# Cross attention: the weighed values turned in 32x32 blocks on VectorE, and each large projection of a step split in two halves

## The chip, the cores and the metric

The kernel runs on one core of one Trainium2 chip. The metric is the device time of one execution in microseconds (us); lower is better. All data are 32-bit floats. TensorE multiplies and turns matrices into PSUM banks, VectorE and ScalarE read and write PSUM and SBUF, GpSimd works on SBUF, and the SyncE queue issues most transfers.

## The reference, cut to what matters

Three sub-layers run one after the other on 8 batches of 256 tokens of width 512: a gated delta rule, a cross attention, and a feed-forward part with a router. The change lies in the cross attention:

```python
q = split_heads(hidden_states @ Wq, q_len)          # 32 heads of 16
k = split_heads(hidden_states @ Wk, q_len)
v = split_heads(hidden_states @ Wv, q_len)
q = q * cos + _rotate_half(q) * sin
k = k * cos + _rotate_half(k) * sin
scores = jnp.maximum(q @ k.T * inv_sqrt_d + attention_mask, finfo.min)
attn_output = softmax(scores) @ v
a_k = split_heads(adapter @ Wk, adapter_len)        # adapter: 256 rows for each batch
a_v = split_heads(adapter @ Wv, adapter_len)
a_scores = jnp.tanh(gate) * softmax(q @ a_k.T * inv_sqrt_d)
attn_output = attn_output + a_scores @ a_v
return attn_output.reshape(bsz, q_len, hid) @ Wo
x = _layernorm(x + cross_attention)                 # then a router score for each token
```

The softmax sums are got by a matmul: between two heads' values stands a block of ones, so each product holds 16 columns of weighed values and 16 columns that repeat the sum. "kind" 0 is the attention over the tokens, kind 1 that over the adapter.

## The kernel before, in words

The main loop of the cross attention (`cross_phase`, lines 982 to 1540) has 128 steps, 16 for each of the 8 batches. Two steps (a group) make one 128-token by 128-feature tile of the attention output; four groups make one query tile, and a batch has two. A step takes four head pairs with one of the two heads each. Below, u is the step and d its number in the batch (u mod 16).

The order of TensorE's work in step u is written out by hand (`pe_all`, lines 1179 to 1233): the scores of step u+1 (four tiles at row groups 0, 32, 64, 96; L1187, banks s0 to s3), the transposes of the first two probability tiles (L1200, into banks t0 and t1), perhaps a piece of other work, the transposes of the other two tiles, perhaps a second piece, and the weighing of step u (32 small matmuls, L1215, into bank o). Those pieces (`early` and `late`, lines 1050 to 1080) make the projections of the next batch, or finish the output of the present one. All of them use one bank, p; a piece may start when the one before has been taken out of it (`wait_taken`).

- early pieces, between the transposes: "norm" at each even d, "turn" at d = 1 and 9, "count" at 3, "qt1" at 7, "kt0" at 11, "kt1" at 13, "spread" at 15.
- late pieces, behind the transposes (or between them where the step has no early piece): x0, x1, q0, q1 at d = 0 to 3, out at 4, qt0 at 5, ak0, ak1, k0, k1, v0, v1, av0, av1 at 6 to 13, out at 14.

q, k, ak are projections (8 matmuls of 128x256, L1123), v, av and out have 4 matmuls of 128x512 (L1129, L1176), qt and kt rotate (L1134), x turns tokens (L1139). A plain matmul of these shows as two instructions in the trace, a transpose as one.

How a group's output comes about before: ScalarE copies bank o to `mixed` (L1309) at the end of each odd step; in the next even step TensorE turns `mixed` with 4 transposes into bank p ("norm", L1161); VectorE takes reciprocals of the sums, multiplies by tanh(gate), scales both kinds and adds them into `attn` (L1333 to L1345). For each query tile TensorE turns `attn` with 4 transposes ("turn", L1165), ScalarE copies that to `attn_t` (L1263), and "out" multiplies it with Wo (L1176). VectorE adds the result to the tokens and takes their statistics (L1359 to L1363).

ScalarE's order in a step: copy of the first turned probabilities (L1282), take of the early piece, second copy, eight exponentials of step u+1 (L1276), take of the late piece, at d = 5 a square root for the layer norm (`root`, L1268), and at odd steps the copy of bank o. VectorE's order: running minimum and mask for the first probability tile of step u+1 (`tops`, L1428), copy (L1437), early take, second tile, second copy, the last two tiles, late take, and at d = 6 `rate` (layer norm and router score of the batch before, L1381 to L1397). At d = 0 VectorE runs `choose` (L1399 to L1416) first. SyncE loads the adapter of the next batch when av1 has been made (L1475, L1476), and GpSimd applies the rotation (L1524 to L1539).

Of the kernel before, what the change touches and what calls it, by code (L numbers as in the profile page):

```python
# [12 lines left out]
P = 128  # L13
# [968 lines left out]
def cross_phase(nc, sem_stack, used, tokens, ctx_dram, mask_dram, weights, tables, tables_loaded, ident, chosen_rows, choice_sources):  # L982
# [4 lines left out]
    with ExitStack() as stack:  # L987
        a = Space(nc, stack, "xa_", sem_stack)
        gains = a.sb("gains", [P, XT, 2, 4])
# [15 lines left out]
        attn = a.sb("attn", [P, 2, D])  # L1005
        attn_t = a.sb("attn_t", [P, KC, P])
# [43 lines left out]
        def early(u):  # L1050

            b, d = divmod(u, HALVES)
            if d % 2 == 0:
                return ("norm", u // 2 - 1) if u else None
            if d == 9:
                return "turn", QT * b
            if d == 1:
                return ("turn", QT * b - 1) if b else None
            if d == 15:
                return ("spread", b - 1) if b else None  # L1060
            if d == 3:
                return ("count", b - 2) if b > 1 else None
            return (EARLY[d], b + 1) if d in EARLY and b + 1 < B else None

        def late(u):

            b, d = divmod(u, HALVES)
            if d == 4:
                return ("out", QT * b - 1) if b else None
            if d == 14:  # L1070
                return "out", QT * b
            return (LATE[d], b + 1) if d in LATE and b + 1 < B else None

        def inner(u):

            return early(u) or late(u)

        def outer(u):

            return late(u) if early(u) else None  # L1080

        TAIL = [("norm", LAST // 2 - 1), ("turn", QT * B - 1), ("out", QT * B - 1), ("count", B - 2), ("spread", B - 1),
                ("count", B - 1)]
        order = [(what, 0) for what in PROJECT]
        for u in range(LAST):
            order += [use for use in (early(u), late(u)) if use]
        order += TAIL
        BY_DVE = ("qt0", "qt1", "kt0", "kt1", "norm", "out", "count")
# [22 lines left out]
        def pe_make(pe, use):  # L1111
            what, at = use
            bank = bank_of[use]
            wait_taken(pe, previous[use])
# [4 lines left out]
            def project(w, half, src):  # L1119
                for h in range(2):  # L1120
                    m = 2 * half + h
                    for k in range(KC):
                        mm = pe.matmul(bank[:, h * S:(h + 1) * S], w[:, k, m * P:(m + 1) * P], src[:, k, :],  # L1123
                                       start=(k == 0), stop=(k == KC - 1))
                return mm

            def values(t, src):
                for k in range(KC):
# [29 lines left out]
            elif what == "norm":  # L1158
                wait(pe, mixed_taken, at + 1)
                for n in range(4):  # L1160
                    mm = pe.transpose(bank[:, n * P:(n + 1) * P], mixed[:, n * P:(n + 1) * P], ident)  # L1161
            elif what == "turn":
                wait(pe, normed, XT * (at + 1))
                for k in range(KC):
                    mm = pe.transpose(bank[:, k * P:(k + 1) * P], attn[:, at % 2, k * P:(k + 1) * P], ident)  # L1165
# [7 lines left out]
            else:  # L1173
                wait_taken(pe, ("turn", at))
                for k in range(KC):
                    mm = pe.matmul(bank[:, :], attn_t[:, k, :], w_o[:, k, :], start=(k == 0), stop=(k == KC - 1))  # L1176
            mm.then_inc(made, 1)

        def pe_all(pe):
# [11 lines left out]
            def turn_probs(v):  # L1191
                for i in range(4):
                    if i == 2 and inner(v):
                        pe_make(pe, inner(v))
# [30 lines left out]
            for u in range(LAST):  # L1225
# [3 lines left out]
                if outer(u):  # L1229
                    pe_make(pe, outer(u))  # L1230
# [4 lines left out]
        def act_take(act, use):  # L1235
# [23 lines left out]
            elif what == "spread":  # L1259
                wait(act, ranked, NC * at)  # L1260
                op = act.activation(score_rows[:, :], bank[:, 0:S], ACT.Copy)
            else:
                op = act.activation(attn_t[:], bank[:].rearrange("p (k n) -> p k n", k=KC), ACT.Copy)  # L1263
# [6 lines left out]
        def act_all(act):  # L1270
# [19 lines left out]
            act.activation(gains[:].rearrange("p t h i -> p t i h"), gate_in[:].rearrange("p (t i h) -> p t i h", t=XT, i=4),  # L1290
                           ACT.Tanh).then_inc(gains_made, 1)
            exps(0)
            for u in range(LAST):
                copy(u, 0)
                if early(u):
                    act_take(act, early(u))
# [3 lines left out]
                if late(u):  # L1300
                    act_take(act, late(u))
# [13 lines left out]
        def dve_take(v, use):  # L1315
# [10 lines left out]
            elif what == "norm":  # L1326
                t, slot = at % XT, at // XT % 2
                blocks = bank[:].rearrange("p (k h i x d) -> p k h i x d", k=2, h=2, i=4, x=2)
                if at == 0:
                    wait(v, gains_made, 1)  # L1330
                wait(v, made, made_at[use])
# [767 lines left out]
```

## Time and profile before

| what | value |
|---|---|
| median of 3 runs | 2974.13 us (2973.5 to 2975.09) |
| the profiled execution, its own time | 2976.63 us |
| its span, first to last instruction | 2974.8 us |
| mean granted TensorE clock | 0.982 of full speed |
| busy over the span | TensorE 94%, weight loads 59%, VectorE 59%, ScalarE 47%, GpSimd 17% |

In the windows shown below the three lines are batch 0, batches 1 to 6, and batch 7 of the loop; behind the busy times (number of instructions in brackets) stand the granted TensorE clock, where 1.00 is full speed, the share of the DMA engines and GB/s.

Most of the page is about the whole span, of which the main loop of the cross attention is a third. So the loop is read from windows and timelines. Busy times of TensorE overlap (matmuls are pipelined): the time a piece takes is read from its start to the start of what follows.

### The profile page before, as it was taken

The page shows a single profiled execution, that of the slowest core. Times are in us where ns is not written, and L with a number is a line of the kernel's source. Part 1 is how long each engine was busy: PE and PEld are TensorE (multiplying, and loading weights), DVE is VectorE, ACT ScalarE, POOL GpSimd, SP SyncE. Part 2 cuts the span into 40 slices and gives each one's busy share as a digit, 9 for nine tenths or more (in the row PEclk, how much of TensorE's full clock was granted, in tenths as well). Part 3 has the DMA queues.
Part 4 walks back from the last instruction along what each step waited for, and adds up shares of the span by engine and source line. Part 5 has one row for each costly group of instructions (what it writes and reads, how often), then busy time and mean ns, then how long its engine had stood idle before and what let it go on. Part 6 is the DMA issues. An engine that isn't in the chain of part 4 may idle for free. (4 is left out here: it accounts for less than half of the span.)

```text
span 2974.8 us, 81892 instructions
## 1 busy us (share of the span) xinstructions
PE 2807.7 (94%) x34646; PEld 1760.9 (59%) x34646; DVE 1748.0 (59%) x4940; ACT 1384.1 (47%) x3313; POOL 503.5 (17%) x626
## 2 busy tenths in 40 slices
PE   6999999999999999999998889999999999977999
PEld 3565656565656555555555566666666566654466
DVE  4555555555555555565656266666767667676533
ACT  3343434343433334343433166666666666664131
POOL 1221212121212121212121210102111010200020
PEclk8999999999999999999998899999999999998999
DMA  5010110101101101011011000000000000000441
GB/s 179 22 45 7 37 33 26 38 13 30 34 13 30 45 19 41 16 31 33 13 30 59 19 12 12 1 12 1 12 12 1 12 1 12 1 2 11 156 208 64
DMA packets 96922, 100.10 MB, mean 34 GB/s; under 512 B 38192, under 2 KB 84528, under 8 KB 95408
## 3 DMA queue, kind: packets, MB, share of 16 engines
q1 hardware_dynamic: 96400, 94.35, 10.0%
q8 instruction: 276, 4.52, 0.6%
q14 instruction: 86, 0.70, 0.1%
q0 software_dynamic: 160, 0.52, 0.0%
HBM read 90.01 MB, written 4.85 MB: 32 GB/s over the span
## 5 line engine op out<-in xcount | busy, mean ns | idle before, releaser
L201 PE MATMUL dr_p<-x_t,dr_w_g 128*128 128x512 f32 x1536 | 740.1, 609 | 11.0 <-DMA dr_w_g<-in_w_in 7.6
L1276 ACT ACTIVATE xa_probs<-xa_probs,xa_low 128x256 f32<-128x256 f32 x1024 | 436.6, 497 | 45.6 <-DVE xa_low L1428 43.6
L201 PEld LDWEIGHTS dr_p<-x_t,dr_w_g 128*128 128x128 f32 x1536 | 268.2, 191 | 226.5 <-issue 216.4
L1428 DVE CUSTOM_DVE_ANT_0 xa_probs<-xa_s,xa_mask 128x256 f32<-128x256 f32 x512 | 213.8, 418 | 263.0 <-PE xa_s L1187 263.0
L1200 PEld LDWEIGHTS xa_t<-ident,xa_probs 128*128 128x128 f32 x2048 | 223.2, 142 | 132.2 <-issue 79.1
L635 DVE SCALAR_TENSOR_TENSOR dr_acc<-dr_p,dr_taps,dr_acc 128x510 f32<-128x510 f32 (+2 forms) x384 | 284.9, 742 | 23.2 <-ACT dr_acc L493 15.2
L1200 PE MATMUL xa_t<-ident,xa_probs 128*128 128x128 f32 x2048 | 286.9, 281 | 7.7 <-DVE xa_probs_t L1437 6.0
L1282 ACT ACTIVATE xa_probs_t<-xa_t 128x512 f32<-128x512 f32 x256 | 152.8, 597 | 250.7 <-PE xa_t L1200 249.1
L1428 DVE CUSTOM_DVE_ANT_0 xa_probs<-xa_s,xa_zeros 128x256 f32<-128x256 f32 x512 | 214.4, 419 | 0.0
L1437 DVE COPY xa_probs_t<-xa_t 128x512 f32<-128x512 f32 x256 | 176.3, 689 | 43.4 <-PE xa_t L1200 29.4
L1215 PE MATMUL xa_o<-xa_probs_t,xa_val 128*32 128x128 f32 x4096 | 140.7, 278 | 44.6 <-DVE xa_probs_t L1437 24.8
L853 POOL TENSOR_TENSOR dr_first<-dr_n_mat,dr_packed 32x256 f32<-32x256 f32 x128 | 92.1, 719 | 503.4 <-DVE dr_n_mat L761 497.8
L493 ACT ACTIVATE dr_acc<-dr_p,dr_taps 128x512 f32<-128x512 f32 x128 | 87.4, 683 | 181.4 <-PE dr_p L201 181.4
L1215 PEld LDWEIGHTS xa_o<-xa_probs_t,xa_val 128*32 128x32 f32 x4096 | 107.1, 110 | 100.1 <-issue 75.2
L1187 PE MATMUL xa_s<-xa_keys,xa_q_pair 32*128 32x512 f32 x1024 | 163.4, 656 | 1.7 <-DVE xa_low L1428 1.0
L1528 POOL TENSOR_TENSOR xa_raw<-xa_raw,cos 128x512 f32<-128x512 f32 x32 | 40.7, 1272 | 689.1 <-DVE xa_by_sin L1324 689.1
L264 PEld LDWEIGHTS dr_g<-dr_yx,dr_f_low 32*32 32x32 f32 x8192 | 83.2, 106 | 109.6 <-issue 61.9
L867 POOL COPY dr_x_half<-dr_yx 32x256 f32<-32x256 f32 x32 | 12.4, 386 | 726.9 <-DVE dr_yx L676 726.9
L378 PE MATMUL dr_m<-dr_wo_g,dr_gated 128*128 128x512 f32 x256 | 127.5, 622 | 0.1
L681 DVE TENSOR_TENSOR tokens<-tokens,dr_m 128x512 f32<-128x512 f32 x64 | 44.0, 687 | 138.5 <-PE dr_m L378 138.5
L254 PEld LDWEIGHTS dr_f<-dr_yx,dr_n_mat 32*32 32x32 f32 x8192 | 82.3, 105 | 64.4 <-DVE dr_yx L769 28.8
L550 ACT ACTIVATE dr_k_tok<-dr_f 128x256 f32<-128x256 f32 x32 | 12.3, 384 | 231.9 <-PE dr_f L243 231.9
(319 smaller groups left out, 4894.8 us busy)
## 6 DMA issues: line engine op xcount, KB each, us to landing
dr_alpha<-alpha_rows SPq DMA_DIRECT2D x64, 254.0 KB, 4.3
dr_w_g<-in_w_in SPq DMA_DIRECT2D x48, 256.0 KB, 5.7
dr_alpha<-alpha_rows SPq DMA_DIRECT2D x32, 256.0 KB, 5.5
ff_wide<-in_fw_qkv SPq DMA_DIRECT2D x8, 1024.0 KB, 14.6
x_t<-in_x_t SPq DMA_DIRECT2D x4, 1024.0 KB, 7.6
tokens<-in_x_tok SPq DMA_DIRECT2D x1, 4096.0 KB, 15.9
dr_wo_g<-in_w_out SPq DMA_DIRECT2D x8, 512.0 KB, 3.8
xa_ctx_b<-in_ctx_t SPq DMA_DIRECT2D x8, 512.0 KB, 3.8
```

The source lines that it names most:

```text
L201: mm = pe.matmul(bank[:, :], w_g[:, k, m, :], x_t[:, k, 2 * S * batch:2 * S * (batch + 1)], start=(k == 0), stop=(k == KC - 1))
L378: mm = pe.matmul(y_banks[n][:, :], gated[:, e, j, c * P:(c + 1) * P], wo_g[:, j, :], start=(j == 0), stop=(j == VH - 1))
L493: act.activation(acc[:, m % 2].rearrange("p e n -> p (e n)"), bank_p[m % 2][:, :], ACT.Copy, scale=taps[:, group, m, TAPS - 1:TAPS]).then_ ...
L635: v.scalar_tensor_tensor(out=to[:, :, d:S], in0=bank[:, :, 0:S - d], scalar=taps[:, group, m, TAPS - 1 - d:TAPS - d], in1=to[:, :, d:S], o ...
L853: op = g.tensor_tensor(first[i], n_mat[i, :, i], packed[i, LOW:LOW + 1, :].to_broadcast([TR, EA, TR]), ALU.mult)
L1187: pe.matmul(bank_s[i][:, :], q_pair[32 * i:32 * i + 32, par, t, h, q * P:(q + 1) * P], keys[32 * i:32 * i + 32, par, t].rearrange("p k n - ...
L1200: mm = pe.transpose(bank_t[i % 2][:, at:at + P], probs[:, v % 3, i, kind, kt * P:(kt + 1) * P], ident)
L1215: mm = pe.matmul(bank_o[32 * i:32 * i + 32, at:at + P], val[:, par, kind, kt, 4 * t + i, h:h + 2], probs_t[:, v % 2, i, kind, kt, :], star ...
L1276: op = act.activation(at, at, ACT.Exp, bias=low[:, v % 3, i, kind:kind + 1], scale=-1.0)
L1282: act.activation(probs_t[:, v % 2, 2 * m].rearrange("p k t n -> p (k t n)"), bank_t[0][:, :], ACT.Copy)\
L1428: op = dve.tensor_tensor_reduce(out=probs[:, v % 3, i, kind, :], in0=bank_s[i][:, kind * S:(kind + 1) * S], in1=mask[:, par, q, :] if kind ...
L1437: dve.tensor_copy(probs_t[:, v % 2, 2 * m + 1].rearrange("p k t n -> p (k t n)"), bank_t[1][:, :]).then_inc(copied[1], 1)
```

## The change

It turns the weighed values on VectorE (`v.transpose`, which turns each 32x32 block in its place) instead of on TensorE. `turn_mixed` turns bank o straight into `mixed`, one 128x512 instruction, in each even step behind the first copy; it takes the place of ScalarE's copy and of the "norm" piece. `share` does the old VectorE arithmetic on `mixed` in SBUF at the end of the same step, and then turns the 128x128 result in blocks once more, straight into `attn_t`, which is doubled; it takes the place of the "turn" piece and of ScalarE's copy. The gate's layout follows.

The pieces are dealt out anew. Each step has a place between the transposes (BETWEEN) and one behind them (BEHIND). The twelve large pieces of a batch (q, k, v, ak, av, out) are made in two halves, at two places that follow each other; the bank is waited for at the first half and handed on at the second. ak0 and ak1 move from d = 6 and 7 to d = 0 and 1, the two outs from 4 and 14 to 6 and 15, `root` from d = 5 to 7, `rate` from 6 to 8. The last group is turned and shared after the loop, behind `choose`.

```diff
-        LATE = {0: "x0", 1: "x1", 2: "q0", 3: "q1", 5: "qt0", 6: "ak0", 7: "ak1", 8: "k0", 9: "k1", 10: "v0", 11: "v1",
-                12: "av0", 13: "av1"}
-        EARLY = {7: "qt1", 11: "kt0", 13: "kt1"}
+        HALF = {"ak0", "ak1", "q0", "q1", "v0", "v1", "k0", "k1", "av0", "av1", "out0", "out1"}
+        BETWEEN = ("ak0", "ak1", "x0", "count", "q0", "q1", "out1", "qt1", "v0", "v1", "k0", "k1", "av0", "kt1", "av1", "out0")
+        BEHIND = ("ak0", "ak1", "x1", "q0", "q1", "qt0", "out1", "v0", "v1", "k0", "k1", "kt0", "av0", "av1", "spread", "out0")
...
-            elif what == "norm":
-                wait(pe, mixed_taken, at + 1)
-                for n in range(4):
-                    mm = pe.transpose(bank[:, n * P:(n + 1) * P], mixed[:, n * P:(n + 1) * P], ident)
-            elif what == "turn":
-                wait(pe, normed, XT * (at + 1))
-                for k in range(KC):
-                    mm = pe.transpose(bank[:, k * P:(k + 1) * P], attn[:, at % 2, k * P:(k + 1) * P], ident)
...
             else:
-                wait_taken(pe, ("turn", at))
-                for k in range(KC):
-                    mm = pe.matmul(bank[:, :], attn_t[:, k, :], w_o[:, k, :], start=(k == 0), stop=(k == KC - 1))
-            mm.then_inc(made, 1)
+                wait(pe, normed, XT * (at + 1))
+                for k in quarters_now:
+                    mm = pe.matmul(bank[:, :], attn_t[:, at % 2, k, :], w_o[:, k, :], start=(k == 0), stop=(k == KC - 1))
+            if last:
+                mm.then_inc(made, 1)
...
-                if u % HALVES == 5 and u > HALVES:
+                if ended(u, 1):
+                    act_take(act, ended(u, 1))
+                if u % HALVES == 7 and u > HALVES:
                     root(act, u // HALVES - 1)
-                if u % 2:
-                    g = u // 2
-                    wait(act, weighed, 8 * (g + 1))
-                    if g:
-                        wait(act, made, made_at["norm", g - 1])
-                    act.activation(mixed[:, :], bank_o[:, :], ACT.Copy).then_inc(mixed_taken, 1)
...
+        def turn_mixed(v, g):
+            wait(v, weighed, 8 * (g + 1))
+            v.transpose(mixed[:, :], bank_o[:, :]).then_inc(mixed_taken, 1)
+
+        def share(v, g):
+            t, tile = g % XT, g // XT
+            blocks = mixed[:].rearrange("p (k h q x d) -> p k h q x d", k=2, h=2, q=4, x=2)
...
+            for h in range(2):
+                op = v.reciprocal(shares[:, :, h], blocks[:, :, h, :, 1 - h, 0])
...
+            v.tensor_tensor(joined[:].rearrange("p q h d -> p h q d"), parts[:, 0], parts[:, 1], ALU.add).then_inc(norm_step, 1)
+            if t == 0 and tile >= 2:
+                wait(v, made, made_at["out", tile - 2])
+            wait(v, norm_step, 4 * g + 4)
+            v.transpose(attn_t[:, tile % 2, t, :], joined[:].rearrange("p q h d -> p (q h d)")).then_inc(normed, 1)
...
                 copy(u, 0)
+                if u and u % 2 == 0:
+                    turn_mixed(dve, u // 2 - 1)
+                if ended(u, 0):
+                    dve_take(dve, ended(u, 0))
                 if u + 1 < LAST:
                     tops(u + 1, 1)
                 copy(u, 1)
                 if u + 1 < LAST:
                     tops(u + 1, 2, 3)
+                if ended(u, 1):
+                    dve_take(dve, ended(u, 1))
+                if u and u % 2 == 0:
+                    share(dve, u // 2 - 1)
+                if u % HALVES == 8 and u > HALVES:
                     rate(dve, u // HALVES - 1)
```

## Rows read from the trace of the kernel before

**Rows 1.** Windows: from:to, length, busy us of PE, PEld, DVE, ACT, POOL; clock.
```profile
1713.14:1843.76 130.62, 121.67 (x1097) 82.33 (x1097) 81.56 (x352) 85.82 (x187) 19.38 (x14) 0.97 0.04 13
1843.76:2612.46 768.70, 727.09 (x6661) 489.85 (x6657) 520.55 (x2200) 521.78 (x1117) 105.77 (x77) 1.00 0.02 7
2612.46:2724.72 112.26, 88.93 (x954) 59.59 (x950) 82.89 (x357) 78.26 (x170) 0.00 (x0) 0.94 0.01 2
```

**Rows 2.** Timeline of TensorE, step u=57 (d=9): start, length, engine, work, idle.
```profile
2172.70 1.14 PE L1187 MATMUL xa_s<-xa_keys,xa_q_pair 32*128 32x512 f32 x8
2173.77 1.09 PE L1200 MATMUL xa_t<-ident,xa_probs 128*128 128x128 f32 x8
2174.70 0.60 PE L1165 MATMUL xa_p<-ident,xa_attn 128*128 128x128 f32 x4
2175.20 1.17 PE L1200 MATMUL xa_t<-ident,xa_probs 128*128 128x128 f32 x8
2176.21 3.62 PE L1123 MATMUL xa_p<-xa_x_b,x_t 128*128 128x256 f32 x16
2179.76 1.08 PE L1215 MATMUL xa_o<-xa_probs_t,xa_val 128*32 128x128 f32 x32
2180.77 1.14 PE L1187 MATMUL xa_s<-xa_keys,xa_q_pair 32*128 32x512 f32 x8
```

**Rows 3.** Timeline, the even step that follows (u=58, d=10; norm and v0).
```profile
2183.27 1.16 PE L1200 MATMUL xa_t<-ident,xa_probs 128*128 128x128 f32 x8
2183.58 0.27 DVE L1333 RECIPROCAL xa_shares<-xa_p 128x8 f32<-128x8 f32 x2
2184.60 0.29 DVE L1345 TENSOR_TENSOR xa_attn<-xa_parts 128x128 f32<-128x128 f32 x1
2184.62 3.70 PE L1129 MATMUL xa_p<-x_t,xa_x_b 128*128 128x512 f32 x8 [0.18 <-DVE xa_parts L1339]
2188.25 1.08 PE L1215 MATMUL xa_o<-xa_probs_t,xa_val 128*32 128x128 f32 x32
```

**Rows 4.** Timeline of TensorE: end of d=15, then d=0 and d=1.
```profile
1970.54 1.08 PE L1215 MATMUL xa_o<-xa_probs_t,xa_val 128*32 128x128 f32 x32 [0.87 <-DVE xa_probs_t L1437]
1971.55 1.39 PE L1187 MATMUL xa_s<-xa_keys,xa_q_pair 32*128 32x512 f32 x8
1979.24 1.44 PE L1187 MATMUL xa_s<-xa_keys,xa_q_pair 32*128 32x512 f32 x8
1985.09 1.39 PE L1187 MATMUL xa_s<-xa_keys,xa_q_pair 32*128 32x512 f32 x8
```

**Rows 5.** Timeline, the step with the square root's table load (d=6).
```profile
2145.59 1.39 PE L1187 MATMUL xa_s<-xa_keys,xa_q_pair 32*128 32x512 f32 x8
2147.11 1.28 ACT L1268 ACT_TABLE_LOAD   x1
2155.71 1.14 PE L1187 MATMUL xa_s<-xa_keys,xa_q_pair 32*128 32x512 f32 x8
```

**Rows 6.** Timeline of VectorE: first and last instruction of choose, then of rate.
```profile
1971.68 0.29 DVE L1402 CUSTOM_DVE_ANT_0 xa_weighted<-xa_score_rows,ident 128x128 f32<-128x128 f32 x1
1974.14 0.16 DVE L1416 TENSOR_SCALAR xa_chosen<-xa_rank 128x2 f32<-128x2 f32 x1
...
2154.16 0.15 DVE L1383 RECIPROCAL xa_ln_den<-xa_ln_den 128x2 f32<-128x2 f32 x1
...
2156.61 0.42 DVE L1396 TENSOR_TENSOR xa_diag<-ident,xa_score 128x256 f32<-128x256 f32 x1
```

**Rows 7.** Groups by line: busy us, mean ns of one, then idle before them.
```profile
L1437 DVE COPY xa_probs_t<-xa_t 128x512 f32<-128x512 f32 x256 | 176.3, 689 | 43.4 <-PE xa_t L1200 29.4
L1538 POOL TENSOR_SCALAR xa_q_pair<-xa_raw,halves 128x512 f32<-128x512 f32 x32 | 49.7, 1564 | 1.6
L1387 DVE TENSOR_SCALAR tokens<-tokens,xa_moments,xa_ln_den 128x512 f32<-128x512 f32 x16 | 8.0, 543 | 0.3
```

**Rows 8.** DMA issues by line: KB each, median us to landing.
```profile
xa_ctx_b<-in_ctx_t SPq DMA_DIRECT2D x8, 512.0 KB, 3.8
```

More of the change, by code:

```diff
@@ L1065, in late @@
[L1065 to L1082, printed above, removed]
+        HALF = {"ak0", "ak1", "q0", "q1", "v0", "v1", "k0", "k1", "av0", "av1", "out0", "out1"}
@@ new lines, in cross_phase, with named @@
+        BETWEEN = ("ak0", "ak1", "x0", "count", "q0", "q1", "out1", "qt1", "v0", "v1", "k0", "k1", "av0", "kt1", "av1", "out0")
+        BEHIND = ("ak0", "ak1", "x1", "q0", "q1", "qt0", "out1", "v0", "v1", "k0", "k1", "kt0", "av0", "av1", "spread", "out0")
+        def named(what, b):
+            if what[:3] == "out":
+                at = QT * b - int(what[-1])
+                return ("out", at) if at >= 0 else None
+            if what in ("spread", "count"):
+                at = b - (1 if what == "spread" else 2)
+                return (what, at) if at >= 0 else None
+            return (what, b + 1) if b + 1 < B else None
@@ new lines, in piece, with ended @@
+        def piece(u, behind):
+            b, d = divmod(u, HALVES)
+            what = (BEHIND if behind else BETWEEN)[d]
+            use = named(what, b)
+            if not use:
+                return None
+            if what not in HALF:
+                return use, True, True
+            whole = list(itertools.chain.from_iterable(zip(BETWEEN, BEHIND)))
+            is_first = whole.index(what) == 2 * d + behind
+            return use, is_first, not is_first
+        def ended(u, behind):
+            made_here = piece(u, behind)
+            return made_here[0] if made_here and made_here[2] else None
@@ L1083, in cross_phase @@
+        TAIL = [("out", QT * B - 1), ("count", B - 2), ("spread", B - 1),
                 ("count", B - 1)]
@@ L1085, in cross_phase @@
         for u in range(LAST):
-            order += [use for use in (early(u), late(u)) if use]
+            for behind in range(2):
+                here = piece(u, behind)
+                if here and here[1]:
+                    order.append(here[0])
         order += TAIL
-        BY_DVE = ("qt0", "qt1", "kt0", "kt1", "norm", "out", "count")
+        BY_DVE = ("qt0", "qt1", "kt0", "kt1", "out", "count")
         made_at, taken_at, bank_of, previous = {}, {}, {}, {}
@@ L1109, in place, with pe_make @@
             return g // (QT * XT) % 2, q, t, v % 2
-        def pe_make(pe, use):
+        def pe_make(pe, use, first=True, last=True):
             what, at = use
             bank = bank_of[use]
-            wait_taken(pe, previous[use])
+            halves_now = [h for h in range(2) if (first, last)[h]]
+            quarters_now = [k for k in range(KC) if (first, last)[k // 2]]
+            if first:
+                wait_taken(pe, previous[use])
             if use == ("x0", B - NC):
@@ L1192, in turn_probs @@
                 for i in range(4):
-                    if i == 2 and inner(v):
-                        pe_make(pe, inner(v))
+                    if i == 2 and piece(v, 0):
+                        pe_make(pe, *piece(v, 0))
                     wait(pe, exped, 4 * v + i + 1)
@@ L1258, in act_take @@
                                     bank[:].rearrange("p (a h d) -> p a h d", a=PAIRS, h=2), ACT.Copy)
-            elif what == "spread":
+            else:
                 wait(act, ranked, NC * at)
                 op = act.activation(score_rows[:, :], bank[:, 0:S], ACT.Copy)
-            else:
-                op = act.activation(attn_t[:], bank[:].rearrange("p (k n) -> p k n", k=KC), ACT.Copy)
             op.then_inc(taken_act, 1)
@@ L1325, in dve_take @@
                                 sin[:, None, :].to_broadcast([P, 2, S]), ALU.mult).then_inc(taken_dve, 1)
[L1326 to L1331, printed above, removed]
-                for h in range(2):
-                    op = v.reciprocal(shares[:, :, h], blocks[:, :, h, :, 1 - h, 0])
-                op.then_inc(norm_step, 1)
-                wait(v, norm_step, 2 * at + 1)
-                v.tensor_tensor(shares[:, 1], shares[:, 1], gains[:, t], ALU.mult).then_inc(norm_step, 1)
-                wait(v, norm_step, 2 * at + 2)
-                for h in range(2):
-                    op = v.tensor_tensor(parts[:, :, h], blocks[:, :, h, :, h, :],
-                                         shares[:, :, h, :, None].to_broadcast([P, 2, 4, XD]), ALU.mult)
-                op.then_inc(taken_dve, 1)
-                wait_taken(v, use)
-                if t == 0 and at >= 2 * XT:
-                    wait(v, made, made_at["turn", at // XT - 2])
-                v.tensor_tensor(attn[:, slot, t * P:(t + 1) * P].rearrange("p (i h d) -> p h i d", i=4, h=2),
-                                parts[:, 0], parts[:, 1], ALU.add).then_inc(normed, 1)
             elif what == "count":
```

59 lines of the change are left out of this document (27 added, 32 removed).

## The prediction

> **What bounds the kernel now.** I looked at the busy slices of the page first: the loop of the cross attention is the part where TensorE shows 8 to 9 tenths. The windows then say how the loop splits: batch 0 takes 130.6 us, batches 1 to 6 together 768.7, that is 128.1 each, batch 7, which has no projections to make, 112.3 [rows 1]. In batches 1 to 6 TensorE is busy 727 of 769 us, VectorE 521, ScalarE 522. So TensorE bounds, and the clock it was granted is 1.00 of full speed, the 2.4 GHz level; in batch 7 it is busy only 79% and does not bound.
>
> The timeline says what a step costs on TensorE, from start to start [rows 2]: scores 1.07 us (2172.70 to 2173.77), two transposed tiles 0.93, "turn" 0.50, two tiles 1.01, k1 3.55, weighing 1.01; sum 8.07, without a hole. The step without pieces is 8.07 - 0.50 - 3.55 = 4.02 us.
>
> Holes are elsewhere, and I name them, since the change moves them:
> - In a step with "norm" the late piece waits until VectorE has scaled out of bank p: from the second transposes (2183.27) to v0 (2184.62) it is 1.35 us in place of 1.01, a hole of 0.34 [rows 3].
> - Step d=0 takes 7.69 us (1971.55 to 1979.24) for 4.02 + 0.50 norm + 0.50 x0 = 5.02 of work, so 2.67 of hole, 0.34 of it the one above: VectorE begins with choose, 2.6 us [rows 4, 6].
> - Step d=1 takes 5.85 for 5.02 of work, 0.8 of hole; where nothing stands behind the transposes (d=15, and d=5 has the same form) the weighing waits 0.87 for VectorE's copy [rows 4].
> - d=6 takes 10.12 (2145.59 to 2155.71) where a norm step with a large piece takes 8.5: ScalarE loads the square root's table (1.28 us) and the other one back, 1.6 of hole [rows 2, 3, 5].
>
> **The change, part by part, for a batch of 1 to 6.** What goes:
> - eight norms on TensorE, 8 x 0.50 = 4.0 us, and the holes behind them, 8 x 0.34 = 2.7;
> - two turns, 2 x 0.50 = 1.0;
> - the hole of the table load, 1.6: `root` is at d=7 now, in whose step and the next TensorE has 1.8 us more in each of the places around it. ScalarE, freed of the copy of bank o too, ends its eight exponentials some 3.9 us behind the third transpose, the root at 5.5, its next copy at 6.1; TensorE wants that copy only at 7.05 (rest of transposes 0.45, half a v 1.8, weighing 1.01, scores 1.07, transposes 0.93, other half 1.8). Were this cover gone, 1.6 would come back;
> - the holes of d=0, 1, 5 and 15: 2.3 + 0.8 + 0.9 + 0.9 = 4.9, less what I put in below.
> Sum 14.2 of 128.1, all of it on TensorE's path. ScalarE's copies of `mixed` and `attn_t` lie beside TensorE's work and bring nothing themselves.
>
> What comes:
> - Splitting. The change from transposes to a projection costs 1.01 - 0.93 = 0.08 us for the 256-wide kind [rows 2], and v0 with its 3.63 is 0.08 above k1's 3.55 [rows 3], so 0.16 for the 512-wide: 6 x 0.08 + 6 x 0.16 = 1.5 us.
> - VectorE. A turn of 128x512 out of PSUM does not occur in the trace. From below the bound is 0.54, a scaling of that shape inside SBUF; from above 1.56, GpSimd's slowest of that shape; the nearest row is the copy of that shape from PSUM, 0.69 [rows 7]. I take 0.69. For the 128x128 turn I take 0.29 as for the addition of that shape [rows 3], bounds 0.2 to 0.5. The old arithmetic takes 1.31 (2183.58 to 2184.89), so `share` is 1.6 and an even step holds 8 x 0.35 (running minima) + 2 x 0.69 + 0.69 + 1.6 = 6.5 us of VectorE in 7.6 of TensorE. In an ordinary even step nothing is late: counting from the start of the scores, VectorE's first tile is done at 2.0, the copy at 2.9, the turn at 3.6, the second tile at 4.3, and the fourth transpose, for which the second copy waits, ends only at 4.75. `share` stands behind the last minima, and only the next step's first tile waits for it (8.6 against 8.9).
> - New holes, where VectorE's queue is longer. d=0: choose and out0's take (three instructions, 1.6) push its first copy to 4.9 where TensorE wants it at 4.25, 0.65. d=9: share and rate (2.9 us [rows 6]) before it, the copy at 5.4 instead of 4.25, 1.15. d=2, now the light step (x0 and x1 alone, 5.0 of work): the turn delays the second copy, 1.05; d=3 behind it 0.5, since bank p and ScalarE's exponentials come late. d=14 has only "spread" behind its transposes, 0.4, and d=15 behind it 0.25. Sum 4.0.
> - DMA and the other queues: the adapter's load is issued when av1 is made, now at d=14 instead of 13, and ak0 wants it at d=0 instead of 6. From issue to need there are some 12 us, it lands in 3.8 [rows 8], so it costs nothing; SyncE's queue holds only the mask behind it, whose condition is older. If it took 20 us, each us over 12 would be on the path. GpSimd's rotations get the same order and steps before.
> So a batch changes by -14.2 + 1.5 + 4.0 = -8.7 us; six of them -52.
>
> Batch 0 loses 7 norms and a turn (7 x 0.84 + 0.5 = 6.4) and its light steps' holes, gains splits and ak0 in the first step, where everything waits and the clock is low: -6. In batch 7 even steps stay light: the norm's 0.50 and VectorE's 1.3 before the second tile give way to a turn of 0.69, but share follows; per pair of steps -0.3, with the root's hole -2 in all, bounds -8 and +5. Behind the loop two sets of four transposes and two ScalarE copies leave the chain and two turns enter it: -1. Sum -52 - 6 - 2 - 1 = -61 us. On the profiled execution, 2976.6 (2.5 us above the median), this is 2915.6; on the median, **2913**.
>
> **A rule weighed.** A copy from PSUM of the turn's shape takes 0.69 us, and four TensorE transposes take 0.50 [rows 2, 7]. The Trainium skill, "VectorE: DVE Perf Modes", section "The three transpose paths", gives 311 ns for a 128x128 turn on VectorE, in 2-byte data, and 390 ns on TensorE; the trace has TensorE's at 0.125 in a stream, so it does not agree with that side, and no row shows the other. An estimate by that page is 4 x 0.311 = 1.24 us for the large turn, which speaks against the change and is the second rival below.
>
> **The rivals.**
> 1. The holes come back elsewhere: only the 5.0 us of TensorE's transposes and half of the rest are won, -5 a batch, -35 in all: 2939. For it: all twelve pieces share bank p, five of them are taken by ScalarE behind its exponentials (d=0, 1, 2, 12, 14) with 0.6 us to spare by my count. Against it: in [rows 2] the same hand-over has no hole.
> 2. The turn is slow, 1.24 to 1.56 us. Then d=0, 2, 9 and 14 are later by 0.9 to 1.0 each, 3.8 a batch, and the eight light even steps of batch 7 by 0.9: 6 x 3.8 + 7 = 30, so 2943.
> 3. It is better balanced than I count: the new holes are small, -12.5 a batch, 2890.
> 4. The other side: VectorE becomes the bound. It is busy 521/6 = 86.8 us of 128.1 a batch, so each of the 8 even steps has room for 5.1 us more before a batch is longer than now. A turn that costs over 4.8 us (seven copies) decides it; at 8 us a batch is 86.8 + 8 x 8.3 = 153, six of them +150, near 3130. For it: only that the trace has no such instruction. Against: no VectorE instruction of that shape in the loop is over 0.7.
> That the change does not do what it says: no; the instructions that it drops are plain in the diff.
>
> **How the numbers follow.** The forecast 60%, rival 1 18%, rival 2 12%, rival 3 7%, rival 4 3%. Range 2893 to 2944: the forecast's own is 2900 to 2926, the lower end goes toward rival 3, the upper takes in rivals 1 and 2. All but rival 4 are faster; about 0.2%, 6 us, is what a measurement of this kernel can tell from no change. Faster 0.94, within 0.02, slower 0.04.
>
> **What would show it.** Right: batches of 119 to 120 us; steps with two halves near 7.6 to 7.8; no wait of TensorE for VectorE's scaling; the turn at 0.69; steps at d=7 and 8 without a table-load hole; holes at d=2, 9 and 0. Wrong: a turn over 1 us, TensorE waiting for bank p at first halves, ak0 waiting for a DMA, or a batch above 123 us.

## The result, and the profile after

The changed kernel takes **2891.06 us** (median of 4 runs, 2885.38 to 2892.61), the kernel before 2973.82 beside it (4 runs, 2971.02 to 2975.09): a ratio of 0.9717, 95% interval 0.9705 to 0.9729. It is faster by 83 us, where 61 were forecast; 2891 lies 2 us below the range's lower end. The profiled execution took 2892.61 us, its span is 84.0 us shorter than before's.

The page's first part, for the whole span: TensorE's share has risen, although it has less to do.

```profile
PE 2747.5 (95%) x34326; PEld 1720.0 (59%) x34326; DVE 1800.7 (62%) x5068; ACT 1328.8 (46%) x3233; POOL 503.5 (17%) x626
```

The windows of the changed kernel, with the columns of [rows 1]: batch 0, batches 1 to 6, batch 7, the stretch from there to the feed-forward part.

```profile
1716.18:1836.18 120.00, 115.50 (x1064) 78.18 (x1064) 87.05 (x365) 80.38 (x181) 19.38 (x14) 0.97 0.05 15
1836.18:2533.07 696.89, 678.84 (x6421) 459.94 (x6417) 558.90 (x2296) 478.81 (x1057) 105.90 (x77) 1.00 0.02 7
2533.07:2639.81 106.74, 81.60 (x914) 53.26 (x910) 88.00 (x367) 73.31 (x159) 0.00 (x0) 0.97 0.01 1
2639.81:2662.37 22.56, 8.04 (x22) 4.06 (x19) 13.22 (x51) 0.68 (x2) 0.00 (x0) 0.77 0.00 0
```

Against [rows 1], batch 0 gives 10.6 us, batches 1 to 6 give 71.8 (12.0 each), batch 7 gives 5.5, and the stretch behind them, 22.56 us, gives nothing (22.60 before). What lies ahead of the loop is 3.0 longer and the rest 0.9; the loop's start lies between 1708 and 1716 us in all traces of this study, whatever the kernel, so that is no effect of the change. In batches 1 to 6 TensorE's busy time falls by 48.2 us and its idle time by 23.6 (from 41.6 to 18.1). The granted clock is 1.00 there in both, the 2.4 GHz level, and takes no part.

Groups by line, window 1600 to 2760, columns as in [rows 7]: the two turns. They take 0.706 us for 128x512 and 0.311 for 128x128.

```profile
L1334 DVE STREAM_TRANSPOSE xa_mixed<-xa_o 128x512 f32<-128x512 f32 x64 | 45.2, 706 | 0.0
L1358 DVE STREAM_TRANSPOSE xa_attn_t<-xa_joined 128x128 f32<-128x128 f32 x64 | 19.9, 311 | 3.2
```

The timeline of TensorE in step u=58 (d=10), whose place before is in [rows 3]. Two halves, no hole, 7.51 us where it was 8.50.

```profile
2141.34 1.14 PE L1183 MATMUL xa_s<-xa_keys,xa_q_pair 32*128 32x512 f32 x8
2142.41 1.09 PE L1196 MATMUL xa_t<-ident,xa_probs 128*128 128x128 f32 x8
2143.34 1.89 PE L1126 MATMUL xa_p<-xa_x_b,x_t 128*128 128x256 f32 x8
2145.07 1.04 PE L1196 MATMUL xa_t<-ident,xa_probs 128*128 128x128 f32 x8
2145.94 1.97 PE L1126 MATMUL xa_p<-xa_x_b,x_t 128*128 128x256 f32 x8
2147.84 1.08 PE L1211 MATMUL xa_o<-xa_probs_t,xa_val 128*32 128x128 f32 x32
2148.85 0.71 PE L1183 MATMUL xa_s<-xa_keys,xa_q_pair 32*128 32x512 f32 x4
```

All steps of one batch (the third), in us, before and after, read from score start to score start:

| d | 0 | 1 | 2 | 3 | 4 | 5 | 6 | 7 | 8 | 9 | 10 | 11 | 12 | 13 | 14 | 15 |
|---|---|---|---|---|---|---|---|---|---|---|---|---|---|---|---|---|
| before | 7.69 | 5.85 | 8.89 | 8.07 | 8.50 | 5.79 | 10.12 | 8.47 | 8.52 | 8.07 | 8.50 | 8.45 | 8.50 | 8.45 | 8.50 | 5.55 |
| after | 8.24 | 7.44 | 5.90 | 6.64 | 7.51 | 6.65 | 7.67 | 7.40 | 7.50 | 8.46 | 7.51 | 6.65 | 7.67 | 6.74 | 6.60 | 7.71 |

Four steps are longer than their work by over 0.6 us: d=0, 2, 7 and 9. The one at d=9, as the timeline shows it: `rate` ends on VectorE at 2136.6, VectorE's first copy of the step comes late, and the transposes of the fourth tile, which go into the bank that it empties, wait.

```profile
2136.18 0.42 DVE L1391 TENSOR_TENSOR xa_diag<-ident,xa_score 128x256 f32<-128x256 f32 x1
...
2137.21 0.68 DVE L1432 COPY xa_probs_t<-xa_t 128x512 f32<-128x512 f32 x1
...
2138.04 0.63 PE L1196 MATMUL xa_t<-ident,xa_probs 128*128 128x128 f32 x4 [0.84 <-DVE xa_probs_t L1432]
```

### The profile page after: what moved, and what is told of

Its sections match the earlier page's. It is cut to its first block and busy times, and to the rows that moved or that the text cites. A ratio compares the mean times of both kernels' runs of the same rounds, so it can differ in the third digit from the quotient of the medians.

```text
span 2890.8 us, 81157 instructions
## 1 busy us (share of the span) xinstructions
PE 2747.5 (95%) x34326; PEld 1720.0 (59%) x34326; DVE 1800.7 (62%) x5068; ACT 1328.8 (46%) x3233; POOL 503.5 (17%) x626
## 3 DMA queue, kind: packets, MB, share of 16 engines
q1 hardware_dynamic: 96400, 94.33, 10.1%
## 5 line engine op out<-in xcount | busy, mean ns | idle before, releaser
L1270 ACT ACTIVATE xa_probs<-xa_probs,xa_low 128x256 f32<-128x256 f32 x1024 | 428.2, 498 | 18.6 <-DVE xa_low L1423 16.3
L1196 PE MATMUL xa_t<-ident,xa_probs 128*128 128x128 f32 x2048 | 280.8, 278 | 22.6 <-DVE xa_probs_t L1432 15.6
L1211 PE MATMUL xa_o<-xa_probs_t,xa_val 128*32 128x128 f32 x4096 | 139.5, 277 | 23.6 <-DVE xa_probs_t L1432 13.8
L265 PE MATMUL dr_g<-dr_yx,dr_f_low 32*32 32x32 f32 x8192 | 98.2, 195 | 24.1 <-DVE dr_f_low L669 20.6
```

The costliest lines, as they stand in the source:

```text
L265: mm = pe.matmul(bank_g[i, n * TR:(n + 1) * TR], f_low[i, n, :], yx[i, 0, n, :], start=True, stop=True)
L1196: mm = pe.transpose(bank_t[i % 2][:, at:at + P], probs[:, v % 3, i, kind, kt * P:(kt + 1) * P], ident)
L1211: mm = pe.matmul(bank_o[32 * i:32 * i + 32, at:at + P], val[:, par, kind, kt, 4 * t + i, h:h + 2], probs_t[:, v % 2, i, kind, kt, :], star ...
L1270: op = act.activation(at, at, ACT.Exp, bias=low[:, v % 3, i, kind:kind + 1], scale=-1.0)
```

## The experiments

Each time is a median of 4 runs unless said otherwise. The kernel before stood beside them at 2974.74 us (experiments 1, 2, 5, 6), 2972.42 (3, 7, 8, 9) and 2973.68 (4, 10).

**1. The turns alone.** All pieces whole and in the steps where they were before; `kt0` and "spread" in their old places, root at d=5, rate at 6. One place differs: qt0, which stood between the transposes of d=5, stands behind them.

```diff
-        HALF = {"ak0", "ak1", "q0", "q1", "v0", "v1", "k0", "k1", "av0", "av1", "out0", "out1"}
...
+        HALF = set()
+        BETWEEN = (None, None, None, "count", None, None, None, "qt1", None, None, None, "kt0", None, "kt1", None, "spread")
+        BEHIND = ("x0", "x1", "q0", "q1", "out1", "qt0", "ak0", "ak1", "k0", "k1", "v0", "v1", "av0", "av1", "out0", None)
...
```

> The turns on VectorE as in the changed kernel, but no piece in halves: the large pieces stand whole behind the transposes at the steps they had in the kernel before, root at d=5 and rate at d=6. Theory: of the 83 us the turns alone bring TensorE's 5.0 us a batch and the 0.34 us holes behind the norms, 7.8 a batch, about 55 us: near 2919, batches near 120.2 us, the hole of the square root's table at d=6 still there (1.3 to 1.6). Rival A (the dealing out in halves brings most of it, the turns only move work): above 2945. Rival B (the turns bring all, halves nothing): near 2891.

Measured: 2950.46 us (2947.2 to 2951.78), ratio 0.9921 (0.9901 to 0.9941). Only 24 us, where I expected over 50: a clear miss. An even step of it, TensorE's timeline:

```profile
2032.56 1.14 PE L1183 MATMUL xa_s<-xa_keys,xa_q_pair 32*128 32x512 f32 x8
2033.63 1.09 PE L1196 MATMUL xa_t<-ident,xa_probs 128*128 128x128 f32 x8
2035.06 1.16 PE L1196 MATMUL xa_t<-ident,xa_probs 128*128 128x128 f32 x8 [0.34 <-ACT xa_probs_t L1276]
2036.06 3.62 PE L1126 MATMUL xa_p<-xa_x_b,x_t 128*128 128x256 f32 x16
2039.61 1.08 PE L1211 MATMUL xa_o<-xa_probs_t,xa_val 128*32 128x128 f32 x32
2040.62 0.71 PE L1183 MATMUL xa_s<-xa_keys,xa_q_pair 32*128 32x512 f32 x4
```

From the first transposes to the second it is 1.43 us, 2033.63 to 2035.06. In [rows 2] it is 0.93 + 0.50, also 1.43. The third tile goes into the bank that ScalarE is still copying; the norm, 0.50, stood exactly in that time. Taken out, it leaves its own length as wait (0.34) and as the run-out of the transposes (1.09 in place of 0.93). Only the hole behind it goes: 8.06 us for this step (d=8) against 8.52. The groups of the transposes in batches 1 to 6, of the kernel before and of this one, with the idle time ahead of them and who ended it, say the same: where the kernel before never waits for ScalarE's copy, this one waits 27.4 us.

```profile
L1200 PE MATMUL xa_t<-ident,xa_probs 128*128 128x128 f32 x1536 | 212.4, 278 | 4.1 <-DVE xa_probs_t L1437 4.1
```

```profile
L1196 PE MATMUL xa_t<-ident,xa_probs 128*128 128x128 f32 x1536 | 216.1, 279 | 39.0 <-ACT xa_probs_t L1276 27.4 <-DVE xa_probs_t L1432 11.4
```

**2. The new places without the halves.** `HALF = set()`; the large pieces whole behind the transposes, and only x0, count, qt1 and kt1 between them.

> The changed kernel with its order of pieces and its turns, but every large piece whole, at the one of its two places that is behind the transposes. Theory: the halves cost TensorE nothing (0.2 us a batch), and what they give is time for VectorE and ScalarE between the transposes: without them the first copy is wanted at 2.45 us of a step in place of 4.25, so d=0 and d=9 have holes of 2.4 and 2.9 us, and d=5, 11 and 14 become light steps of 5.9; batches near 123 us, 45 us slower than the changed kernel, near 2936. Rival B (halves bring nothing): within 5 us of 2891.

Measured: 2953.44 us (2949.55 to 2955.79), ratio 0.9933 (0.9912 to 0.9954). It is 17 us slower than I expected: I had counted VectorE's lateness, and not the wait for ScalarE's copy between the transposes. The new order is worth nothing by itself against experiment 1; in this order the halves are worth 62 us, all of the rest. A third form, the whole large piece between the transposes and nothing behind them, wasn't built. The kernel before has it at d=5 with qt0: ScalarE's copy is covered, but the weighing waits 0.88 us for VectorE's copy, more than the 0.50 of the empty place, so by that step it is no better (worked out, not shown). The groups of TensorE for batches 1 to 6, of this kernel (first) and of the changed one (second); the last part is idle time ahead of the group and who ended it:

```profile
L1196 PE MATMUL xa_t<-ident,xa_probs 128*128 128x128 f32 x1536 | 217.6, 280 | 38.8 <-ACT xa_probs_t L1276 24.9 <-DVE xa_probs_t L1432 13.9
L1211 PE MATMUL xa_o<-xa_probs_t,xa_val 128*32 128x128 f32 x3076 | 104.1, 275 | 9.6 <-issue 9.4
```

```profile
L1196 PE MATMUL xa_t<-ident,xa_probs 128*128 128x128 f32 x1536 | 209.2, 277 | 11.4 <-DVE xa_probs_t L1432 11.1 <-ACT xa_probs_t L1276 0.3
L1211 PE MATMUL xa_o<-xa_probs_t,xa_val 128*32 128x128 f32 x3076 | 104.1, 275 | 6.6 <-issue 6.6
```

The waits for ScalarE's copy are gone, 24.9 to 0.3 us, those for VectorE's copy fall by 2.8, and those ahead of the weighing by 3.0. Together they are 30 of the 49.5 us between the two kernels in these batches; the other 19 are busy time of the same instructions, which run out with nothing behind them where the place is empty (1.09 us in place of 0.93, experiment 1).

**3. TensorE work put into the empty place.** Experiment 1, with four transposes of the identity into bank p (nobody reads them) in the eleven steps of a batch that have nothing between the transposes.

```diff
+                    elif i == 2:
+                        before_it = [p[0] for w in range(v) for p in (piece(w, 0), piece(w, 1)) if p]
+                        wait_taken(pe, before_it[-1] if before_it else ("av1", 0))
+                        for n in range(4):
+                            pe.transpose(bank_p[:, n * P:(n + 1) * P], ident, ident)
```

> The kernel of e1_turn_only with four transposes of the identity into bank p, read by nobody, in each step that has nothing between its transposes: 0.50 us more TensorE work in 11 to 16 steps a batch, some 5.7 us a batch, 45 in all. Theory: where nothing stands between the transposes, the third waits for ScalarE to empty the first bank (0.5 us), so what was taken away with the norms came back as a wait there; filled again the time is that of e1_turn_only (2950) within 6 us. Rival (TensorE work between the transposes is always paid): 2990 to 2995.

Measured: 2946.09 us (2943.66 to 2951.62), ratio 0.9911 (0.9894 to 0.9927). 11 x 0.50 = 5.5 us of TensorE work a batch cost nothing. The windows of batches 1 to 6, of experiment 1 and then of this one:

```profile
1838.77:2588.23 749.46, 697.83 (x6420) 461.79 (x6416) 560.07 (x2296) 488.60 (x1058) 106.08 (x77) 1.00 0.02 7
```

```profile
1836.94:2587.03 750.09, 721.30 (x6688) 491.12 (x6685) 559.57 (x2296) 488.62 (x1057) 106.00 (x77) 1.00 0.02 7
```

Busy is 23.5 us up, the time 0.6. Idle falls from 51.6 to 28.8, and of it the waits for ScalarE's copy ahead of the transposes from 27.4 to 3.9.

**4. The same load in the changed kernel**, ahead of each of the nine pieces of a batch that begin between the transposes.

```diff
+                        if piece(v, 0)[1]:
+                            wait_taken(pe, previous[piece(v, 0)[0]])
+                            for n in range(4):
+                                pe.transpose(bank_p[:, n * P:(n + 1) * P], ident, ident)
```

> The changed kernel with four transposes of the identity into bank p, read by nobody, ahead of each piece that begins between the transposes (d=0, 1, 2, 3, 6, 7, 12, 13, 15): nine times the 0.50 us of TensorE that one norm took, 4.5 us a batch. Theory: with halves in place TensorE's work is paid in full wherever the step has no hole (d=1, 6, 12, 13, 15: 2.5 us a batch) and is swallowed where VectorE is late anyway (d=0, 2, 3, 7): +15 in batches 1 to 6, some 3 in batch 0 and 1 in batch 7, near 2910. Rival (TensorE's turns cost nothing here either, as in e5_filled): 2891 to 2895. Rival (all is paid): 2927.

Measured: 2907.89 us (2903.87 to 2912.99), ratio 0.9781 (0.9758 to 0.9803), 17 us slower than the changed kernel. Here the same instructions are paid: in steps without a hole (d=1, 6, 12, 13, 15) 0.43 or 0.44 us each, at d=3 0.2, where a hole was left (d=0, 2, 7) nothing. So TensorE bounds the changed kernel except in its last holes. That also prices the old norm: it would cost now what it did not cost in experiment 1. The halves with all turns left on TensorE, the rival to the change as a whole, weren't built. This run is the nearest to it: nine sets of four transposes a batch in place of the eight norms and two turns, with the rest of the change kept, are still 66 us faster than the kernel before.

**5. The turn done twice.** A second turn of 448 of the 512 columns into a tile that nobody reads.

```diff
...
+            if g:
+                wait(v, spared, g)
+            v.transpose(spare[:, :], bank_o[:, 0:448]).then_inc(spared, 1)
```

> The changed kernel with a second turn of 448 of the 512 columns of bank o in each even step, into a tile that nobody reads: 0.6 us more VectorE work in 64 steps, 39 us in all. Theory: VectorE has room in ordinary steps, so only d=0, 2, 7, 9, 14 of each batch and the light steps of batch 7 get longer: +2.5 a batch, +20 in all, near 2911. Rival D (VectorE already sets the pace of every even step): +39, near 2930. Rival E (VectorE off the path everywhere): below 2896.

Measured: 2907.05 us (2902.91 to 2911.95), ratio 0.9784 (0.9763 to 0.9805); 16 us more than the changed kernel, about as expected. The group shows 0.64 us for one, 64 of them are 41 us of VectorE, of which 16 reach the end, but not where I expected them. A batch from the third on gets 0.9 us longer: d=0 by 0.10, d=1 by 0.29, d=2 by 0.53. The steps at d=7, 9 and 14 take what they took; at d=8 VectorE still waits 0.61 us for the transposes between its turn and its second copy (changed kernel, 2013.90), which takes the longer turn up. Batches 1 to 6 make 5 of the 16 us, batch 0 makes 2 and batch 7 some 7. This tells what a turn of 1.3 us, as in the second rival, would have made of the time: some 16 us, not 30.

**6. Share moved to the odd steps**, and choose to d=1, to take VectorE's peaks down.

```diff
-                if u % HALVES == 0 and u > HALVES:
+                if u % HALVES == 1 and u > 2 * HALVES - 1:
                     choose(dve, u // HALVES - 2)
...
-                if u and u % 2 == 0:
+                if u > 2 and u % 2:
                     share(dve, u // 2 - 1)
```

> The changed kernel with share at the end of each odd step (from 3) in place of the even one, and choose at d=1 in place of d=0. Theory: the holes at d=0 (0.73 us), d=7 (0.75) and d=9 (0.95) come from VectorE's queue alone and go: -2.2 us a batch from batch 2 on, -12 us in all, near 2879. Rival C (these holes are TensorE's waits for ScalarE's exponentials or for bank p): no change, 2891, or slower where share at odd steps makes other holes.

Measured: 2902.0 us (2896.52 to 2905.29), ratio 0.9759 (0.9737 to 0.9782). A miss: 11 us slower than the changed kernel in place of faster. The three holes are gone (d=0 7.44, d=7 6.7, d=9 7.5), but d=6 takes 9.6 and d=12 9.2. The timeline of VectorE and GpSimd at the end of d=5:

```profile
1999.03 0.27 DVE L1344 RECIPROCAL xa_shares<-xa_mixed 128x8 f32<-128x8 f32 x2
1999.20 1.27 POOL L1529 TENSOR_TENSOR xa_raw<-xa_raw,cos 128x512 f32<-128x512 f32 x1 [45.31 <-DVE xa_by_sin L1311]
1999.34 1.16 DVE L1347 TENSOR_TENSOR xa_shares<-xa_shares,xa_gains 128x8 f32<-128x8 f32 x1
2000.53 1.57 DVE L1350 TENSOR_TENSOR xa_parts<-xa_mixed,xa_shares 128x128 f32<-128x128 f32 x2
2000.55 1.39 POOL L1535 TENSOR_TENSOR xa_raw<-xa_raw,xa_by_sin 128x512 f32<-128x512 f32 x1
```

The 128x8 product ends at 2000.50, just behind GpSimd's multiplication (2000.47). In the changed kernel it takes 0.167 us on average, here 1.16. Of the two products of 128x128 the first, issued 0.02 us ahead of GpSimd's addition, takes 0.29; the second takes 1.36 and ends at 2002.10, just behind that addition (2001.94). TensorE waits 1.77 us at d=6 for the copy of VectorE that stands behind all this. The Trainium skill, "SBUF — State Buffer", section "Who interferes with whom", says that a VectorE instruction with two SBUF inputs contends with a GpSimd instruction that reads SBUF, and that the order of issue decides which of them blocks. The trace agrees for GpSimd's multiplication and addition, with 1.16 against 0.167 us. Beside GpSimd's scaling that follows, VectorE's addition takes 0.75 in place of 0.29 and ends 0.7 us ahead of the scaling, so there it is slowed and not held to the end.

**7. The rotation cut down.** Experiment 6, with GpSimd's rotation on 8 of 256 columns from batch 2 on, so the queries and keys are not the reference's there.

```diff
-                        at = raw[:, 2 * m:2 * m + 2, :]
+                        few = S if b < 2 else 8
+                        at = raw[:, 2 * m:2 * m + 2, 0:few]
...
```

> The kernel of e3_balanced, with GpSimd's rotation applied to 8 of each 256 columns from batch 2 on (the rest of keys and queries is left as it was, so the attention's values are not the reference's): GpSimd's instructions become short, their order and waits stay. Theory: share at d=5 and d=11 was slow in e3 (a gain product took 1.16 us in place of 0.17) because GpSimd's rotation ran beside it; without it the steps d=6 and d=12 fall from 9.6 and 9.2 to 7.7, -3.4 us a batch: near 2882. Rival (share at odd steps is late by its order alone): 2902 as e3.

Measured: 2882.34 us (2879.47 to 2885.59), ratio 0.9697 (0.968 to 0.9713). The steps d=6 and 12 are back at 7.7; in batch 0 of the loop, where the queries and keys of batch 1 get the full rotation, they still take 10.1 and 9.2. The 128x8 product's group, window 1700 to 2560, in experiment 6 and in this one:

```profile
L1347 DVE TENSOR_TENSOR xa_shares<-xa_shares,xa_gains 128x8 f32<-128x8 f32 x56 | 23.3, 415 | 1.9
```

```profile
L1347 DVE TENSOR_TENSOR xa_shares<-xa_shares,xa_gains 128x8 f32<-128x8 f32 x58 | 11.7, 201 | 2.0
```

So the contention is shown: by the two ratios it costs 18 us in this order of the work. The changed kernel, with share at even steps, doesn't meet it: its mean is 0.167.

**8. The table load taken out of the kernel before.** `root` with Exp in place of Sqrt, which leaves the layer norm's scale wrong.

```diff
-            act.activation(ln_den[:, b, :], moments[:, b, :, 1], ACT.Sqrt, ...)
+            act.activation(ln_den[:, b, :], moments[:, b, :, 1], ACT.Exp, ...)
```

> The kernel before with the exponential in place of the square root in root (the layer norm's scale, and what follows from it, is left wrong), so ScalarE loads no other table in the loop. Theory: the hole of d=6 was 1.6 us of table loads in each of seven batches: -11 us, near 2963. Rival (the hole comes from rate on VectorE, not from the table): 2974.

Measured: 2966.66 us (2958.88 to 2969.91, 10 runs), ratio 0.9974 (0.9965 to 0.9984). The step d=6 falls from 10.12 to 8.79: the loads cost 1.3 us a batch and not 1.6, and about 6 to 8 us in all, where I expected 11. The kernel before shows the way by which they reached TensorE: at d=6 the norm waits 1.32 us for `mixed`, whose copy stood behind the root on ScalarE.

**9. The three peaks moved apart**, in the changed kernel: share stays at even steps; choose at d=1, root at 8, rate at 9, and the statistics of out1 at the end of d=7.

```diff
...
-                if u % HALVES == 8 and u > HALVES:
+                if u % HALVES == 9 and u > HALVES:
                     rate(dve, u // HALVES - 1)
```

> The changed kernel with share left in even steps, choose at d=1, root at d=8, rate at d=9, and the statistics of out1 measured at the end of d=7 in place of d=6. Theory: VectorE's extra work stands where neither share nor GpSimd's rotation does, so the holes of d=0 (0.73), d=7 (0.75) and d=9 (0.95) go and no others come: -2.4 us a batch, -13 in all, near 2878. Rival: moved work makes new holes as in e3, 2885 or more.

Measured: 2879.73 us (2875.63 to 2885.68), ratio 0.9686 (0.9668 to 0.9704), as expected in time; the holes of d=7 (6.74 now) and d=9 (7.50) are gone, that of d=0 has moved to d=1, which takes 8.3.

**10. The same, and d=0's share moved behind the tiles of d=1.**

```diff
-                if u and u % 2 == 0:
+                if u % 2 == 0 and u % HALVES or u % HALVES == 1 and u > 1:
```

> The kernel of e8_moved with the share of d=0 put at the end of d=1, behind choose, so that neither stands before the other's copies. Theory: the one hole that e8 kept (0.87 us at d=1, from share at the end of d=0 with choose behind it) goes: -0.87 in five batches and a little in the last, near 2875. Rival: it turns up at d=2, a light step: 2880.

Measured: **2870.68 us** (2867.82 to 2873.99), ratio 0.9647 (0.9628 to 0.9665), the best of the study: 20 us below the changed kernel. The window of its batches 1 to 6:

```profile
1835.27:2518.49 683.22, 676.26 (x6420) 460.40 (x6416) 560.30 (x2296) 475.99 (x1057) 105.88 (x77) 1.00 0.03 7
```

and the group of its transposes there:

```profile
L1196 PE MATMUL xa_t<-ident,xa_probs 128*128 128x128 f32 x1536 | 205.9, 276 | 0.3 <-ACT xa_probs_t L1276 0.3
```

Of 11.4 us of wait ahead of the transposes 0.3 are left, and TensorE idles 7.0 of 683. The other 6.6 are ahead of the weighing, as in the changed kernel, 0.78 at d=2 and 0.32 at d=14. The profile names no releaser for them, but the weighing starts there 0.1 us behind the end of VectorE's second copy (1968.80 to 1968.90 at d=2), so d=2 keeps its hole: the turn stands ahead of that copy.

## Why the prediction was right and wrong

The likeliest case was the right one in kind, and its size was off: 83 us in place of 61. The step of the prediction that failed most is its term for splitting the large pieces. By its own steps, a batch of 1 to 6 (12.0 us won, 8.7 forecast):

- *The turn's price.* Taken as 0.69 and 0.29 us, measured 0.706 and 0.311. The estimate by the Trainium skill, "VectorE: DVE Perf Modes", section "The three transpose paths", gave 4 x 0.311 = 1.24 us for the large turn, and the trace doesn't agree: four times the columns take 2.3 times as long. The page's 311 ns for 128x128 in 2-byte data is what the trace shows too, here in 4-byte data. I also overlooked rows of the kernel before: its delta rule has 160 such turns of 128x256, and this is the group of 128 of them. Twice 0.445 is 0.89 us for 128x512, an estimate from rows inside SBUF that speaks against the 1.24 to 1.56 of the second rival and the 4.8 of the fourth.

```profile
L676 DVE STREAM_TRANSPOSE dr_yx<-dr_yx 128x256 f32<-128x256 f32 x128 | 57.0, 445 | 4.4
```

- *The norm and its hole*, 4.0 + 2.7: about right as a sum, but the reason was incomplete. I booked the norm's 0.50 as won by the turn. Experiments 1 and 3 show that it covered ScalarE's copy and costs nothing to keep or to lose while the place stays empty; in these experiments it is the halves that turn it into time. The forecast for the whole change was saved because both come together, which is luck; and that is why the expectation for experiment 1 was 31 us too low.
- *Splitting*, forecast +1.5: **the term that failed most**, measured about -0.5, so 2.0 us a batch. In d=10 the two halves cost 7.51 - 4.02 = 3.49 us where the whole piece is 3.55; the 512-wide at d=6 7.67 - 4.02 = 3.65 against 3.63. The largest savings are at d=0 and 1 (7.44 without a hole, against 4.02 + 3.55 = 7.57), d=8 (7.50 against 7.65) and d=9 (7.51 without a hole, against 7.62). I had added a change of kind at each half. The timeline shows that transposes behind a projection take 0.87 (2145.07 to 2145.94) in place of 1.01, which pays it back and more.
- *Holes of before*, forecast 9.2 (2.7 + 1.6 + 4.9): about 10.0. I had left out, for one, d=2, 8.89 for 4.02 + 0.50 + 3.55 = 8.07 of work and the 0.34 of the norm. The table load's part of it was 1.3, not 1.6.
- *New holes*, forecast 4.0, measured 3.9. Three are read against the same step without its hole in experiments 6, 9 and 10: d=0 0.80 (0.65 forecast), d=9 0.95 (1.15), and 0.66 at d=7, which I didn't name. The others are read against the sum of the step's work: d=2 0.9 (1.05), d=3 0.3 (0.5), d=14 0.25 (0.4), d=15 0.05 (0.25). So the total is right partly by luck, since the one that I left out stands in for what the others lack. At d=7 VectorE adds and measures out1's result, and the share of d=6 stands before its copies (timeline of the changed kernel; the share ends at 2004.25):

```profile
2001.07 0.68 DVE L1325 TENSOR_TENSOR tokens<-tokens,xa_p 128x512 f32<-128x512 f32 x1
...
2003.94 0.31 DVE L1358 STREAM_TRANSPOSE xa_attn_t<-xa_joined 128x128 f32<-128x128 f32 x1
...
2004.84 0.69 DVE L1432 COPY xa_probs_t<-xa_t 128x512 f32<-128x512 f32 x1
...
2005.67 0.63 PE L1196 MATMUL xa_t<-ident,xa_probs 128*128 128x128 f32 x4 [0.50 <-DVE xa_probs_t L1432]
...
2009.85 1.28 ACT L1262 ACT_TABLE_LOAD   x1
...
2012.82 1.04 PE L1196 MATMUL xa_t<-ident,xa_probs 128*128 128x128 f32 x8
```

- *The root at d=7*: the last two lines above. The table load is still there, 1.28 us, and the transposes that need ScalarE's copy come without a wait; d=8 is 7.50. As forecast.
- *The adapter's load* at d=0 brings no wait, as forecast.
- *Batch 0*, forecast -6, measured -10.6. Its first step, with ak0 in it, is 2.25 us longer (12.54 before, 14.79 after), and the other fifteen 12.9 shorter. I had left out most of what I counted for the steady batch there.
- *Batch 7*, forecast -2, measured -5.5: two light steps as d=1 and 2 take 7.38 + 6.77 before and 6.04 + 6.15 after, more than the 0.3 per pair that I had. *Behind the loop*, forecast -1, measured 0.

Together, in the batch of the table: 5.0 of transposes and 10.0 of holes go, 3.9 of holes come and splitting gives 0.5, which makes the 11.6 measured. The mean of the six batches is 0.35 higher, since one batch of the kernel before is 1.3 us longer than its neighbours, and batch 1 of the changed kernel has no hole at d=0 (7.44). Against the forecast the six are 6 x 3.3 = 20 us better (71.8 against 52), of which splitting makes 12, the holes of before 5, the higher mean 2 and the new holes 1; batch 0 makes 4.6, batch 7 3.5, behind the loop -1, the stretches outside the loop -3.9: 84 - 61 = 23.

**The rivals.** The first (holes come back, 2939) is refuted for the whole change, 2891; but what it says happens when the turns are made alone, 2950, by another wait than it named: ScalarE's copy of the bank, not bank p. The second (a slow turn) is refuted by 0.706 us and its price was too high (experiment 5). The third, 2890, is the time that was measured, but not for its reason: the new holes were as large as counted, and splitting and the old holes made the difference. The fourth would have needed a turn of 4.8 us. Its engine does set the remaining holes, though: moving VectorE's work (experiments 9 and 10) brought 20 us more.

How much of the 62 us between experiment 2 and the changed kernel is from filling the empty places and how much from the thinner run of work between VectorE's copies isn't separated by a run; a step's arithmetic (8.06 to 7.51, of it 0.50 the place and 0.05 the rest) puts about 12 x 0.50 x 6 = 36 us of it in the first, for the twelve empty places a batch of experiment 2. That is worked out, not shown.

## What to carry to other kernels

Work that stands between two uses of a double buffer may be free because it covers the copy out; before counting it as won when it goes, look whether the next instruction on that engine would wait as long, and have something else to put there. A large piece cut in two halves is a good filler for such places, if the accumulation and the hand-over of its bank allow it. When one engine bounds and another sets its holes, place the second one's lumps (here choose, rate, share) one to a step.

## What the runs showed of the hardware

- A 32x32-block turn of 128x512 32-bit floats from PSUM on VectorE takes 0.706 us, about as long as a copy of that shape (0.69); of 128x448 from PSUM 0.64, of 128x256 inside SBUF 0.445, of 128x128 inside SBUF 0.311.
- VectorE's products with both inputs in SBUF, beside GpSimd's 128x512 multiplication and addition, are stretched from 0.167 to 1.16 us (128x8) and from 0.29 to 1.36 (128x128), where they start behind it. Reads of PSUM by VectorE beside GpSimd were not: the 128x512 copy at 2003.81 of experiment 6, in the time of the scalings, takes 0.69, and so does the one at 2006.72 of the changed kernel, in the time of the multiplication.
- Eight transposes take 0.93 us of TensorE when other work follows, 1.09 when nothing does, and from their start to the start of what follows 0.87 when a projection ran before them, 1.01 when four other transposes did.
